# The opening of an eight-expert attention and routing kernel written anew, with three steps of the group body put in another order

## The reference

```python
mod = (_silu(L0_c) @ L0_wmod).reshape(L0_c.shape[0], 6, 1, -1)
sa, ca, ga, sb, cb, gb = (mod[:, 0], mod[:, 1], mod[:, 2], mod[:, 3], mod[:, 4], mod[:, 5])
...
h = _layernorm(x, axis=-1) * (1 + ca) + sa
x = x + ga * _L0_attn_ref(h, ...)
h = _layernorm(x, axis=-1) * (1 + cb) + sb
x = x + gb * _L0_ffn_ref(h, ...)
```

```python
M = M * b_t[:, :, None, None] + (k_t[:, :, None] * v_t[:, None, :])[:, None]
Z = Z * b_t[:, :, None] + k_t[:, None, :]
num = jnp.einsum('bd,bcde->be', q_t, M)
den = jnp.einsum('bd,bcd->b', q_t, Z) + EPS
```

## Time and profile before

| | us |
|---|---|
| median of 3 runs | 318.68 (315.65 to 319.35) |
| the profiled execution, its own time | 318.16 |
| its span, first to last instruction | 316.3 |
| mean granted TensorE clock | 0.857 |
| PE busy | 259.2 (82%) |
| DVE busy | 198.4 (63%) |
| ACT busy | 122.1 (39%) |
| POOL busy | 87.8 (28%) |

### The profile page before, as it was taken

How to read it: one execution, slowest core, us unless ns; L and a number is a source line. 1 busy time by engine, 2 the same in 40 slices (tenths; PEclk the granted TensorE clock), 3 DMA queues, 4 the chain that set the end, 5 groups by cost and what they waited for, 6 DMA issues and landing times.

```text
span 316.3 us, 11186 instructions
## 1 busy us (share of the span) xinstructions
PE 259.2 (82%) x4698; PEld 193.8 (61%) x4698; DVE 198.4 (63%) x786; ACT 122.1 (39%) x274; POOL 87.8 (28%) x102
## 2 busy tenths in 40 slices
PE   4977696969988999789987998965999999999900
PEld 2655455856646786467844666423778887888800
DVE  5288749687786939697496676605753444325594
ACT  4368344564356734385332013300324233342300
POOL 0002001300000320604205125550245544464530
PEclk9999687589977569996599586996999999999975
DMA  6998000000000000100001001114043523430466
GB/s 220 323 384 342 5 0 2 5 4 2 4 3 4 4 19 2 43 16 4 21 4 36 21 21 37 44 43 127 7 136 97 159 61 117 143 99 26 134 220 221
DMA packets 18053, 24.97 MB, mean 79 GB/s; under 512 B 2663, under 2 KB 11256, under 8 KB 18002
## 3 DMA queue, kind: packets, MB, share of 16 engines
q1 hardware_dynamic: 14290, 18.97, 18.2%
q0 software_dynamic: 2368, 4.24, 4.1%
q10 hardware_dynamic: 1344, 1.05, 1.0%
HBM read 12.62 MB, written 12.15 MB: 78 GB/s over the span
## 4 chain that ended last, share of the span: by engine, by line
PE 51%; DVE 18%; issue 7%; DMA 4%; ACT 2%; POOL 1%; DVEq 0%; POOLq 0%
PE ps L1814 9%; PE ps L1460 9%; PE ps L1831 7%; PE ps L1558 6%; PE ps L1465 3%; PE ps L1600 3%; DVE arena L985 2%; PE ps L1565 2%; DVE last_p L1386 2%; PE ps L1495 2%; PE ps L1640 2%; PE ps L1655 1%; PE ps L1585 1%; DVE z L1087 1%; DMA arena<-pair_out 1%
## 5 line engine op out<-in xcount | busy, mean ns | idle before, releaser
L924 ACT ACTIVATE arena<-ps 128x385 f32<-128x385 f32 (+1 forms) x64 | 27.6, 439 | 68.3 <-PE ps L1814 67.6
L665 POOL DMA_INDIRECT pair_out<-arena,meta x40 | 39.2, 980 | 51.1 <-DVE arena L1377 35.0
L611 POOL DMA_INDIRECT dispatched<-row,idx x32 | 31.6, 986 | 61.3 <-PE ps L1565 37.0
L1831 PE MATMUL ps<-w2t,arena 128*128 128x128 f32 x320 | 42.3, 281 | 1.7 <-DVE arena L1377 1.7
L1831 PEld LDWEIGHTS ps<-w2t,arena 128*128 128x128 f32 x320 | 39.9, 191 | 3.9 <-DVE arena L1377 3.0
L1814 PE MATMUL ps<-arena,w1t 128*128 128x256 f32 (+1 forms) x128 | 39.6, 452 | 1.1 <-issue 1.1
L1465 PE MATMUL ps<-later_b,ident_b 128*128 128x512 bf16 x120 | 33.7, 418 | 0.0
L634 POOL TENSOR_TENSOR arena<-arena,ex 128x256 f32<-128x256 f32 x16 | 9.5, 624 | 79.8 <-PE ps L1585 57.8
L1814 PEld LDWEIGHTS ps<-arena,w1t 128*128 128x128 f32 x128 | 23.9, 199 | 11.6 <-issue 3.2
L1558 PE MATMUL ps<-v,wts 32*32 32x9 f32 x2048 | 24.9, 183 | 7.1 <-issue 4.5
L1558 PEld LDWEIGHTS ps<-v,wts 32*32 32x32 f32 x2048 | 23.2, 123 | 12.2 <-issue 11.8
(11 more groups left out here) (186 smaller groups left out, 437.8 us busy)
## 6 DMA issues: line engine op xcount, KB each, us to landing
dispatched<-fill SPq DMA_DIRECT2D x12, 260.0 KB, 5.7
pair_out<-zero SPq DMA_DIRECT2D x6, 512.0 KB, 8.0
arena<-dispatched SPq DMA_DIRECT2D x8, 325.0 KB, 3.0
w1t<-in_w SPq DMA_DIRECT2D x8, 256.0 KB, 2.6
w2t<-in_w SPq DMA_DIRECT2D x8, 256.0 KB, 3.0
arena<-pair_out SPq DMA_DIRECT2D x4, 512.0 KB, 5.4
const<-in_constants SPq DMA_DIRECT2D x1, 803.0 KB, 5.5
X<-in_x SPq DMA_DIRECT2D x1, 768.0 KB, 6.6
```

The lines of the kernel that those rows point to most:

```text
L611: pool.indirect_dma_start(disp_d, bass.IndirectOffsetOnAxis(ap=idx[:, p.g, t, k:k + 1], axis=0), row[:, p.g, t, k, :], None, bounds_check= ...
L665: pool.indirect_dma_start(pair_d, bass.IndirectOffsetOnAxis(ap=meta[:, u, a, 0:1].bitcast(U32), axis=0), orow[:, u, a, :], None, bounds_ch ...
L924: a_.activation(hid[:, u, f, c0:c0 + cn], ps[:, k % 4, 0:cn], ACT.Silu).then_inc(hid_done[u].sem, 1)
L1831: m = mm(row_bank(u, a)[:, 0:P], hid[:, u, f, 1 + a * P:1 + (a + 1) * P], w2t[:, u, f, :], start=(f == 0), stop=(f == FT - 1))
```

## The change

It has two parts. The opening:

- the identity matrix is loaded after the modulation weights;
- the four products of the modulation vectors are split: two ahead of `norm_T(0)`, two behind it, in another bank;
- group 0's projections stand ahead of its decay logits, which get their own bank (T6), and its exponents get banks 0 and 1, so that they wait neither for the raw copies nor for the transposed queries' bank;
- ACT takes `softplus(0)` after the projections and values, `key_factors(0)` ahead of `query_factors(0)`, and `keys_T` ahead of `query_factors_T`;
- `key_factors` waits for the first half of the exponents only;
- `keep_streaming` is cut from 8 + 5 to 4 + 2 + 5 ahead of the first scores, and from 8 to 2 ahead of `norm_T(1)`;
- `gate_tables` goes from the head of body 0 to the opening, ahead of `clipped_logits(1)`.

The bodies: on PE `adds(g, 3)` and `query_T(n)` stand ahead of `scores(g, 3)`, and the transposes of the query factors are a step of their own behind it. On DVE `states(g, 3)` stands ahead of `queries_T(n)`, and `mask_states(g, 3)` and `gated(g, 3)` ahead of `normed(g, 2)`. Since qx has one buffer, `queries_T(n)` now waits until `scores(g, 3)` has been made. Ahead of `ranks` there are 5 streaming products in bodies 0 to 2, where there were none (3 in body 2).

```diff
 def key_factors(g):
-    act.wait_ge(expo_ps.sem, expo_ps.now(g))
+    act.wait_ge(expo_ps.sem, expo_ps.now(g, 1))
...
 def queries_T(g):
     dve.wait_ge(tq.sem, tq.now(g))
+    if g:
+        dve.wait_ge(scored.sem, scored.now(g - 1))
...
 def dve_body(g, more):
     n, m = g + 1, g + 2
-    if g == 0:
-        gate_tables()
...
     normed(g, 1)
+    states(g, 3)
     if more:
         queries_T(n)
-    states(g, 3)
+    mask_states(g, 3)
+    gated(g, 3)
     if more:
         normed(g, 2)
-    mask_states(g, 3)
-    gated(g, 3)
...
+            gate_tables()
             clipped_logits(1)
...
     attention(g, 1)
-    scores(g, 3)
     adds(g, 3)
     if more:
         query_T(n)
+    scores(g, 3)
+    if more:
+        query_factors_T(n)
         attention(g, 2)
...
     route(whole(g))
-    if m == GROUPS:
-        keep_streaming(ps[:, 0, :], 3)
+    keep_streaming(ps[:, 0, :], 5)
     ranks(whole(g))
...
 norm_T(0)
+modulation(3, ((0, 3), (1, 4)))
+project(0, 0, TG)
 pe.wait_ge(s_biasrow, 1)
 logit_bias(0)
 decay_logits(0)
-project(0, 0, TG)
...
-keep_streaming(ps[:, 3, :], 8)
+keep_streaming(ps[:, 3, :], 2)
 query_T(0)
 key_T(0, (T6, T7))
+query_factors_T(0)
...
 attention(0, 0)
-keep_streaming(T4, 8)
+keep_streaming(T4, 2)
 norm_T(1)
```

More of the change, by code:

```diff
@@ L888, in _ @@
             layer_input(0)
-            softplus(0)
             projections(0)
@@ L892, in _ @@
             values(0)
+            softplus(0)
             block_values(0, 0, 1)
             feature_exp(0)
+            key_factors(0)
             query_factors(0)
-            key_factors(0)
             block_factors(0)
+            keys_T(0, T6)
             query_factors_T(0)
-            keys_T(0, T6)
             block_values(0, 1, BPT)
@@ L1276, in _, with modulation @@
             v_.tensor_copy(vecs[:], ps[:, 1, 0:ROWV]).then_inc(s_vecs, 1)
[L1277 to L1282 removed]
+            def modulation(n, bank):
+                j = 2 * n
+                mc = ps[:, bank, 0:2 * B].rearrange("p (j b) -> p j b", b=B)
+                dve.wait_ge(s_modc, n + 1)
+                for b in range(B):
+                    v_.tensor_copy(modc[:, j:j + 2, b * GPB:(b + 1) * GPB], mc[:, :, b:b + 1].to_broadcast([P, 2, GPB])).then_inc(s_modc_sb, 1)
+                dve.wait_ge(s_modc_sb, 3 * n + 2)
+                v_.tensor_scalar(modc[:, j + 1:j + 2, :], modc[:, j + 1:j + 2, :], 1.0, None, ALU.add).then_inc(s_modc_sb, 1)
+            modulation(0, 0)
             dve.wait_ge(s_csilu, 1)
             v_.tensor_copy(c_rep[:], c_silu[:].unsqueeze(2).to_broadcast([P, B, P])).then_inc(s_crep, 1)
[L1285 removed]
+            modulation(1, 3)
             dve.wait_ge(s_const, 16)
@@ L1452, in _, with modulation @@
             pe.wait_ge(s_csilu, 1)
-            for n, j in enumerate((0, 1, 3, 4)):
-                f = mm(ps[:, 0, n * B:(n + 1) * B], wmod[:, j * DM:(j + 1) * DM], c_silu[:], start=True, stop=True)
-            f.then_inc(s_modc, 1)
+            def modulation(bank, js):
+                for n, j in js:
+                    f = mm(ps[:, bank, n * B:(n + 1) * B], wmod[:, j * DM:(j + 1) * DM], c_silu[:], start=True, stop=True)
+                f.then_inc(s_modc, 1)
+            modulation(0, ((0, 0), (1, 1)))
             pe.wait_ge(s_ident, 16)
@@ L1474, in logit_bias @@
             def logit_bias(g):
-                mm(Z_ps if g else T5[:, 0:TG * HC], ones_row[:], bias_row[:], start=True, stop=False, skip_group_check=True)
+                mm(logit_bank(g), ones_row[:], bias_row[:], start=True, stop=False, skip_group_check=True)
             def decay_logits(g):
@@ L1481, in decay_logits @@
                 for t in range(TG):
-                    f = mm((Z_ps if g else T5)[:, t * HC:(t + 1) * HC], hT[:, t * P:(t + 1) * P], wall[:, 3 * DM:WALL], start=False, stop=True,
+                    f = mm(logit_bank(g)[:, t * HC:(t + 1) * HC], hT[:, t * P:(t + 1) * P], wall[:, 3 * DM:WALL], start=False, stop=True,
                            skip_group_check=True)
@@ L1486, in project @@
             def project(g, lo, hi):
+                pe.wait_ge(hT_done.sem, hT_done.now(g))
                 for t in range(lo, hi):
@@ L1490, in project @@
                         pe.wait_ge(raw_done.sem, raw_done.now(g, t - 1))
-                    elif t and g < 2:
+                    elif t and g == 1:
                         pe.wait_ge(zclamp.sem, zclamp.now(g))
@@ L1497, in exponents @@
             def exponents(g):
-                pe.wait_ge(raw_done.sem, raw_done.now(g))
+                if g:
+                    pe.wait_ge(raw_done.sem, raw_done.now(g))
                 pe.wait_ge(rate_done.sem, rate_done.now(g))
                 rv = rate[:].rearrange("p t h -> p (t h)")
-                mm(T4[:, 448:448 + BPT], rv, K["blk"], start=True, stop=True).then_inc(sum_ps.sem, 1)
+                across, within = decay_banks(g)
+                mm(across[:, 448:448 + BPT], rv, K["blk"], start=True, stop=True).then_inc(sum_ps.sem, 1)
                 for i in range(NSUB):
-                    f = mm(T5[:, i * TG * HC:(i + 1) * TG * HC], K["gk"][:, i * P:(i + 1) * P], rv, start=True, stop=True)
+                    f = mm(within[:, i * TG * HC:(i + 1) * TG * HC], K["gk"][:, i * P:(i + 1) * P], rv, start=True, stop=True)
                 f.then_inc(expo_ps.sem, 1)
@@ L1508, in exponents @@
                 for i, n in enumerate(("own", "cq", "ck")):
-                    mm(T4[:, i * TG * HC:(i + 1) * TG * HC], K[n], rv, start=True, stop=True)
-                mm(T4[:, 3 * TG * HC:3 * TG * HC + TG * 2 * BPT], K["spread"], sums[:].rearrange("p a b -> p (a b)"),
+                    mm(across[:, i * TG * HC:(i + 1) * TG * HC], K[n], rv, start=True, stop=True)
+                mm(across[:, 3 * TG * HC:3 * TG * HC + TG * 2 * BPT], K["spread"], sums[:].rearrange("p a b -> p (a b)"),
                    start=True, stop=True).then_inc(expo_ps.sem, 1)
@@ L1516, in query_T @@
                 pe.wait_ge(phi_done.sem, phi_done.now(g))
-                pe.wait_ge(dec_done.sem, dec_done.now(g))
+                if g:
+                    pe.wait_ge(dec_done.sem, dec_done.now(g))
                 for t in range(TG):
@@ L1536, in key_T @@
                     pe.wait_ge(fqx_done.sem, fqx_done.now(g))
+                else:
+                    pe.wait_ge(fk_done.sem, fk_done.now(g))
                 for t in range(TG):
@@ L1762, in _ @@
             f.then_inc(s_modb, 1)
+            pe.wait_ge(s_const, 16)
+            pe.wait_ge(s_trib, 3)
+            keep_streaming(ps[:, 3, :], 4)
+            exponents(0)
             pe.wait_ge(s_small, 32)
-            keep_streaming(ps[:, 3, :], 8)
+            keep_streaming(ps[:, 3, :], 2)
             query_T(0)
             key_T(0, (T6, T7))
+            query_factors_T(0)
             pe.wait_ge(s_gate, 2)
```

35 lines of the change are left out of this document (17 added, 18 removed).

## The result

The changed kernel took 302.84 us (median of four, 302.13 to 311.07) beside 319.01 for the kernel before; the ratio is 0.9515, 95% interval 0.9432 to 0.9598. Its executions spread by 9 us: those at 302 to 304 us had a mean granted clock of 0.895 to 0.905, the profiled one, 311.07 us, had 0.866. So I show next to it the profile of a later execution, 307.34 us. On another chip, six executions gave 306.73 us against 317.50: 0.965 (0.959 to 0.971). The forecast was 307.7, faster.

What follows compares the result with a forecast made beforehand. The prediction took one long alternation of PE and DVE, each waiting for the other, to bound the kernel. Terms -0.7 - 0.9 - 3.2 + 1.1 - 7.6 + 0.3 = -11.0 gave 307.7 us beside the median; range 304.5 to 311.5, with rivals 302.5 to 313.5.

Steps and rivals of the forecast that it cites:

- rival 1: Better clock: idle times ending full-clock stretches shrink, half-clock tails in bodies 1 and 2 go; -4, 303.7 us; chance 0.12.
- Opening: Up to the first scores: hT sooner, projections directly behind it, ACT losing idle time; -0.7 us, bounds 0 and -1.25.
- Clipped logits: First attention to group 1's clipped logits: fewer streaming products, gate tables just fit DVE's idle time; -0.9 us, bounds 0 and -1.0.
- Tables and clock: Body 0: tables moved out let rotations and sums start sooner, -3.2 us; full clock comes one stretch later, +1.1.
- its own warning sign: Named beforehand as showing the forecast wrong: projections of group 1 taking over 5 us.
- Middle of the bodies: Bodies 0 to 2: states off the path to the next attention, `queries_T` sooner; -2.8, -2.8, -2.0, sum -7.6 us.
- Streaming ahead of ranks: Five streaming products in PE's 1.80 us idle time, hidden or 0.45 too long; +0.3 us for three bodies, bounds 0 and +1.4.
- Rival 2: Opening gives little: clock returns later, table and streaming terms end near -1, first scores gain nothing; 311.7 us; chance 0.13.
- Rival 3: PE's instruction supply bounds the middle of the bodies: only about 2.5 of 7.6 us remain; 312.8 us; chance 0.20.
- 24 products further back: Body 1: the 1.39 us PE stop would still fall inside the scores in the new order, and not grow.
- Rival 4: Slower: without six streaming products body 0 loses its full-clock stretches; +13.6 against -11.0, 321.3 us, up to 329; chance 0.05.

Runs made afterwards that it cites:

- the last run: The whole change unaltered, timed again against the kernel before on one chip: 306.73 us (six executions), ratio 0.965.
- The order alone: Kernel before with only the new order in the middle of the bodies; opening and streaming unchanged, tables in body 0: 312.26 us, ratio 0.984.
- the opening alone: New opening with the gate tables moved, bodies in the old order, old streaming ahead of ranks, against the kernel before: 313.67 us, ratio 0.984.
- the instruction counts: Changed kernel with opening streaming products split into more, narrower ones, against the kernel before: quarters 308.03 us, ratio 0.9705; eighths 314.66 us, 0.981.

## Why the prediction was right, step by step

The sign and the places are as forecast, and the sum is too: -11.0 against -10.8 in the execution of 307.34 and -10.8 in the medians of the last run. That it comes so near is in part luck. Term by term the opening gave more and the middle of the bodies less than forecast, and the two errors cancel. And the three times that the whole was timed gave -16.2, -8.4 and -10.8 by their medians. The first four executions, three of them near 303, lie some 5 us below the forecast and outside its own range of 304.5 to 311.5; that is the side of rival 1, whose price (-4) fits, but no profile of such an execution shows its place.

- **Opening.** -0.7 forecast; -2.3 and -3.0 measured. I took half of ACT's idle time; it gave nearly all, and the keys ahead of the factors the rest. Mis-sized: the upper bound of 1.25 came from one idle time, while hT, the keys and the factors each moved.
- **Clipped logits.** -0.9 forecast, -0.5 and 0.0 measured. The tables fit as worked out, and DVE is the bound there: statistics until 37.25, then 3.88 of tables without a wait. So what the opening gave above its forecast was in part used up here.
- **Tables and clock.** -3.2 + 1.1 = -2.1 forecast; -1.6 and -2.6 measured. The mechanism is as told (rotations of 1.43, nothing waited for at L1534), and its own warning sign came too: projections over 5 us. The clock cost 2.2 us of PE time (5.34 against 3.16) in one execution and 1.2 (4.39) in the other, where I took 1.1. With eight products instead of two it costs nothing and L1534 comes as soon: the six products and the clock cancel. I had called the opening mostly at half clock because its projections took 4.27 us. The granted clock reads 1.00 there, from 8.0 to 16.0 us, although the eight matrix instructions of the logits take 1.92 us at 10.01, as they do in the change at 0.50, and 1.08 at 42.83, where the clock is 1.00 too; why, no run shows.
- **Middle of the bodies.** From y of tile 1, where the forecast began its sum, to attention 3 the three bodies took 8.8, 8.8 and 8.0 us before, and 6.9, 6.5 and 5.9 in the profile of 311.07: -1.8, -2.3, -2.1 = -6.2, against -2.8, -2.8, -2.0 = -7.6. In the execution of 307.34 it is -6.4. The order alone gave some 5 by time. The waits are gone as told; what is missing lies on PE. In body 0 it is the 1.0 of the stop. In body 1 the middle lies wholly at half clock (attention 2 takes 1.89), PE runs through without a pause, and attention 3 begins 0.56 behind y of tile 2. Where PE is not late, DVE is the bound: states, `queries_T`, mask, weights and norm, 5.9 us.
- **Streaming ahead of ranks.** +0.3 forecast, about -1.3 measured, small.

Rival 2 (the opening gives little) is out by the opening alone at 0.984; in its working -0.9 - 3.2 had become -3.9 in place of -4.1, which changes its price by 0.2. Rival 3 was half right: PE's supply is real, shown by the instruction counts and the packets, and takes about 1.0 us of the middle of body 0. But it does not take the 5 of its price, because DVE is busy for nearly as long. I had read the stop in body 1 right, and was wrong on where it would go, that it would stay in the scores, "24 products further back": it stands in attention 2, behind its 69th product, in three profiles of the change, and is missing in the one where PE is at half clock. The Trainium skill (Runtime: NRT & Kernel Launch, "Instruction fetch mechanics") calls the crossing mostly hidden. These runs agree for most of the 37 packets of the queue, since far fewer stops than packets stand in the profiles, but not in dense small products, where PE stands for 1 to 2.45 us. Rival 4 (slower by lost clock) did not come: the full-clock stretch of body 0, 45.6 to 59.0, is longer than the one it replaces (41.6 to 51.8), only later.

Still open: what decides between executions near 303 and near 310. For 3 of these microseconds it is the granted clock behind attention 3 of body 2; why the grant differs from one execution to the next, and where the rest lies, no run here tells. The mean clock alone is not the answer: the kernel before with the streaming alone took 317.44 us in an execution at 0.907.

## What to carry to other kernels

Where two engines alternate, count the waits of the one that is waited for, and move what it can do early into its largest idle time; here the place of eight table instructions was worth some 2 us, as much as the new order of one body. An idle time elsewhere on the chain is a loss only by what its cover lacks: the stop of 2.00 us on PE cost about 1.0, the one of 1.17 nothing. And an edit's worth is to be read part by part over several executions, since their spread (8 us) is nearly as large as the change. A sum that comes out right has to be read term by term as well: here two errors of over 1 us each cancelled.
